# Causal attention of 16 heads: the turning products of a finished half move behind the first score product of the next step

## The reference, cut to what matters

```python
qkv = lora_linear(hidden_states, w_attn, b_attn, la_attn, lb_attn)
q, k, v = heads of 16, 16 wide each
k = fake_quant(k, kv_scale, kv_zero_point)
v = fake_quant(v, kv_scale, kv_zero_point)
scores = einsum('bhqd,bhkd->bhqk', q, k) / sqrt(16)
scores = where(causal, scores, -inf)
attn = softmax(scores, axis=-1)
out = einsum('bhqk,bhkd->bhqd', attn, v)
return lora_linear(out, w_proj, b_proj, la_proj, lb_proj)
```

## Time and profile before

| what | value |
|---|---|
| median of three runs | 2819.18 us (2816.0 to 2820.63) |
| the profiled execution | 2812.74 us, span 2811.1 us, mean granted clock 0.831 |
| PE busy | 2037.8 us (72%) |
| DVE busy | 1663.0 us (59%) |
| ACT busy | 1044.9 us (37%) |
| POOL busy | 875.2 us (31%) |
| exponentials L867 | 384, 206.4 us busy |
| score products L779 | 384, 118.9 us busy |
| value products L797 | 768, 95.7 us busy |

### The profile page before, as it was taken

One profiled execution on the slowest core, in us unless ns is written; L12 is line 12 of the kernel. 1 busy time (PEld: TensorE's weight loads), 2 busy tenths in 40 slices (PEclk: granted clock), 3 DMA queues, 4 the chain that ended last, 5 costly groups with the idle time before them and its releaser, 6 DMA issues. The chain is left out here.

```text
span 2811.1 us, 39533 instructions
## 1 busy us (share of the span) xinstructions
PE 2037.8 (72%) x14369; PEld 1068.1 (38%) x14429; DVE 1663.0 (59%) x3104; ACT 1044.9 (37%) x1811; POOL 875.2 (31%) x1078
## 2 busy tenths in 40 slices
PE   7688887885579966899998834444829694259992
PEld 4333335224322242233333522232414374148991
DVE  4766644684368755777786157995683404445442
ACT  3377762341024423777777121111210312134330
POOL 2122220351224514565653101231461000332225
PEclk9699988898789987999999656556969796579996
DMA  5100000000100012000000220000101100352113
GB/s 181 45 20 23 24 7 25 1 1 10 27 1 1 1 37 117 24 27 33 29 30 13 89 81 8 2 2 16 62 30 41 36 1 5 127 167 77 47 48 99
DMA packets 79687, 113.42 MB, mean 40 GB/s; under 512 B 17861, under 2 KB 57809, under 8 KB 78481
## 3 DMA queue, kind: packets, MB, share of 16 engines
q1 hardware_dynamic: 70913, 99.04, 10.5%
q0 software_dynamic: 3664, 9.32, 1.1%
q10 hardware_dynamic: 4928, 2.62, 0.3%
HBM read 78.65 MB, written 32.05 MB: 39 GB/s over the span
## 5 line engine op out<-in xcount | busy, mean ns | idle before, releaser
L1167 DVE TENSOR_REDUCE a_mx<-a_SM 128x2 f32<-128x1024 f32 x256 | 300.5, 1218 | 81.0 <-PE a_SM L1041 80.7
L1150 ACT ACTIVATE a_P<-a_ST 128x512 f32<-128x512 f32 x512 | 295.7, 596 | 123.2 <-PE a_ST L1067 122.2
L867 ACT ACTIVATE a_P<-a_ST,a_scale 128x512 f32<-128x512 f32 (+3 forms) x384 | 206.4, 589 | 81.6 <-PE a_ST L779 80.2
L882 DVE TENSOR_REDUCE a_mx<-a_SM 128x2 f32<-128x1024 f32 (+1 forms) x192 | 176.2, 952 | 66.2 <-PE a_SM L744 37.3
L1067 PE MATMUL a_ST<-a_Q,a_K 98*128 98x512 bf16 (+1 forms) x456 | 171.6, 391 | 19.0 <-ACT a_P L1150 9.9
L1085 PE MATMUL a_OP<-a_P,a_V 128*32 128x256 f32 (+1 forms) x1792 | 157.4, 423 | 25.2 <-issue 9.6
L714 POOL TENSOR_SCALAR_AFFINE_SELECT a_P<-a_P 128x128 f32<-128x128 f32 (+1 forms) x256 | 77.7, 308 | 239.8 <-ACT a_P L867 238.7
L779 PE MATMUL a_ST<-a_Q,a_K 50*128 50x512 bf16 (+3 forms) x384 | 118.9, 357 | 24.0 <-ACT a_P L867 23.6
L3188 DVE TENSOR_TENSOR experts_hl<-work 128x512 bf16<-128x512 f32 x92 | 83.8, 970 | 88.6 <-POOL work L3038 88.6
L3038 POOL CAST work<-work 128x512 bf16<-128x512 f32 x92 | 73.6, 840 | 199.9 <-PE experts_py L3122 185.3
L1067 PEld LDWEIGHTS a_ST<-a_Q,a_K 98*128 98x128 bf16 (+1 forms) x512 | 51.4, 101 | 197.0 <-ACT a_P L1150 95.8
(11 more groups left out here) (548 smaller groups left out, 4835.1 us busy)
## 6 DMA issues: line engine op xcount, KB each, us to landing
work<-L_ffn_W SPq DMA_DIRECT2D x16, 1024.0 KB, 6.4
conv_tab<-dft_tables SPq DMA_DIRECT2D x8, 1024.0 KB
bias_hankel<-bias_rows SPq DMA_DIRECT2D x16, 448.0 KB, 3.4
a_K<-a_k_parts SPq DMA_DIRECT2D x96, 64.0 KB
a_Q<-a_q_parts SPq DMA_DIRECT2D x96, 64.0 KB
expert_rows<-zeros SPq DMA_DIRECT2D x1, 5888.0 KB, 22.8
experts_xs<-expert_rows SPq DMA_DIRECT2D x23, 256.0 KB, 2.9
expert_results<-params SPq DMA_DIRECT2D x23, 256.0 KB, 2.2
```

What stands on the lines that cost most here:

```text
L867: act.activation(Pr[:, s % 2, u, j, c0:N], ST[:, u, c0:N], ACT.Exp, scale=kscale[:, 0:1]).then_inc(exp_done, 1)
L882: dve.tensor_reduce(mx[:, g % 2, qt, k0 // N, :], SM[:, c % 2, :, 0:kn], AX.X, ALU.max).then_inc(mx_read, 1)
L1150: act.activation(Pr[:, s % 2, u, j, :], ST[:, (4 * s + x) % 2, :], ACT.Exp, scale=scale).then_inc(exp_done, 1)
L1167: dve.tensor_reduce(mx[:, g % 2, qt, k0 // N, :], SM[:, c % 2, :, :], AX.X, ALU.max).then_inc(mx_read, 1)
```

## The change

The call of `outputs` moves from behind the values of a step to the next step, behind its first score product:

```diff
                     scores(s, 0)
+                    if event(outputs_at, s - 1):
+                        outputs(*event(outputs_at, s - 1))
                     maxima(lo, cut[0])
                     if event(rows_at, s):
                         rows(*event(rows_at, s))
 ...
                     scores(s, 2)
                     if s:
                         values(s - 1)
-                    if event(outputs_at, s):
-                        outputs(*event(outputs_at, s))
                     scores(s, 3)
                     maxima(cut[1], hi)
```

## The result

The changed kernel is slower: 2834.6 us in the median of 18 runs (2822.7 to 2861.7), against 2818.4 us (2812.6 to 2828.8) before. The ratio is 1.0069, with a 95% interval of 1.0048 to 1.0090 (it is taken over all runs; the quotient of the medians is 1.0057). The sign was forecast; the size of +7.4 us was not: it is +16 us in the medians, more than twice as much, and +18.7 us between the two profiled executions (span 2829.8 against 2811.1 us). The spread is new too. The runs of the kernel before lie 16 us apart, those of the changed one 39 us.

What follows compares the result with a forecast made beforehand. Neither TensorE nor ScalarE alone was the bound; the second score product set the step. 14 x 0.31 + 14 x 0.26 + 0.52 = 8.50 us, less 1.06 in the last group, gave +7.4: 2826.6 us, range 2817 to 2835.

Steps and rivals of the forecast that it cites:

- +7.4 us: Whole run: 8.50 us of delay over 29 turns, less 1.06 us gained in the last group; chance 0.66.
- The second score product sets the step: In both placements ScalarE waits for this product, so the 1.01 us freed ahead of the last exponential only moves.
- The turn moves back by 0.31 and 0.26 us: Products turning a finished half (L809) start behind two score products: 0.31 us later for second halves, 0.26 for first.
- Rival 1: The turn's first weight load runs beside the scores: shifts of 0.12 and 0.07 us, +1.9 us, 2821.1; chance 0.18.
- VectorE's read ends last: Ahead of the maxima rows (L763), which wait for it: 14 second-half and 15 first-half turns pass on 0.31 and 0.26 us.
- Rival 2: ScalarE sets the step, so its idle time is regained: 28.3 us over 28 exponentials, about 2791; chance 0.07.
- rival 3: The turn waits out the scores and pays a weight load: 0.60 us a turn, +16.3 us, 2835.5; chance 0.09.
- the one unseen cost: TensorE's step from scores to turn, shown by no row: bounds 0.04 to 0.60 us, 0.31 and 0.26 taken.
- a cause I have not counted: A clock row below 1.00 in the middle groups of the profile after; no size given.

Runs made afterwards that it cites:

- the first fill: Changed kernel plus repeats of the second score product ahead of the rows, while TensorE waits for VectorE's read: 2832.8 us against 2817.5, ratio 1.0060.

## Why the prediction was right in its mechanism and wrong in size

- *The second score product sets the step, not the last one of the step before.* Right: ScalarE's idle time moved and didn't vanish, and the version that frees this product is the one that gains.
- *The turn moves back by 0.31 and 0.26 us.* Right: 0.32 and 0.26 us. The Trainium skill, TensorEngine Tiling (Array Packing), Key Properties, says that a change of tiling mode drains the engine. The trace agrees so far as the turn starts only 0.07 us ahead of the score product's modelled end. The 0.32 us hold the score product itself, and no run has the same pair without a change of mode, so what a drain costs by itself isn't shown.
- *Rival 1, the weight load hides.* It fell: the turn's load starts together with its first product, both at 242.04, and the shifts are 0.32 and 0.26 us, not 0.12 and 0.07.
- *VectorE's read ends last, the delay passes on in full, 14 and 15 times.* Right: 7.2 us against 7.4, and the kernel with a longer read confirms the path one to one.
- *Rival 2 and rival 3.* The gain did not come. The measured time lies near rival 3 (+16.2 against +16.3 us), for another reason: no drain is longer than taken.
- *The step that failed is the total of +7.4 us, which has no term for TensorE's clock.* I took the step from scores to turn for "the one unseen cost", and the clock for given because 14 groups had 1.00. I named it as "a cause I have not counted", without a price. In its place the runs showed a clock that falls to half in the middle groups: +17.2 us in the profile, about +8 us in the median of this kernel and up to +27 us in its neighbours. Rows of the kernel before had part of the price: in its last group, at half clock, value products of 512 columns last 1.93 us instead of 1.06. What they did not have is how often it would happen.
- *The range of 2817 to 2835 us holds the 2834.6 us by luck.* Its upper part came from a longer drain, which did not occur.
- *A slip without effect:* the recorded "0.71 us" for VectorE's read is 0.74 and 0.73 us by the rows beside it, and no term uses it.

What the runs leave open is why the small delay makes the clock fall at all. Both kernels with the rows behind the second score product have a shorter pause in step 3 (0.28 us at a period of 18.61, at most 0.1 at 18.77, instead of 0.65), which fits that they are free of falls. But the kernel before, at 18.72 us, has the pauses of steps 1 and 3 at their full length and no fall, and the kernel with the first half moved, at 18.97, has the same pauses and five. TensorE's busy share doesn't rank them either: the first fill has 17.44 of 19.32 us and three falls, the kernel with turn and rows later 16.73 of 18.61 and none. That successive groups must line up in some way fits these numbers, but no run here changed only that, so it isn't shown.

## What to carry to other kernels

Products moved out of a wait pay only if what follows them isn't itself waiting for their reader: follow the chain from the moved piece to the next product that the idle engine needs. A stage whose TensorE has many pauses of half a microsecond may hold the full clock only by luck: here small delays cost two to seven times their length. Give a range for it, and look at the granted clock of each run before explaining a median. Repeated products in the pause where the clock falls are a cheap test, and here most of a cure: the median came back to that of the kernel before, the spread of 25 us stayed.

## What the runs showed of the hardware that was not expected

- The granted clock fell from 2.4 to 1.2 GHz in groups whose longest pause of TensorE is 0.65 us (26 falls in six profiles, behind pauses of 0.29 to 0.65 us).
- Two repeats in each of the pauses at steps 1, 3 and 4, on top of the fill ahead of the rows, took the falls in the middle groups from four and six (two profiles of the changed kernel) to none in one profile, without lengthening the period of 19.3 us; the fill ahead of the rows alone, 1.4 us behind the turn's start, left three.
- With the same instructions ahead of it, the clock rose at different times: the first turn of the changed kernel starts at 121.59 us in one profile and at 126.14 in the other.
- Score products of half the rows and a turn of all rows hardly overlap: the turn starts 0.07 us ahead of the modelled end of the 0.39 us product (241.72 to 242.04), and a score product 0.07 us ahead of the modelled end of the turn (249.25 to 250.26 in the kernel before).
